# Moving one group of transposed scores ahead of the weighted sums in every second slot of a decoder-layer kernel

## What is computed

```
q = _qdq(x) @ _qdq(wq).T + bq
kv = cond @ wkv.T + bkv                      # cond: 16 x 1500 x 256
attn = softmax(einsum('bnhd,bmhd->bhnm', q, k) * scale, axis=-1)
o = einsum('bhnm,bmhd->bnhd', attn, v).reshape(B, N, C)
```

## Time and profile before

| what | value |
|---|---|
| time, three runs | 882.23, 886.67 and 886.75 us; median 886.67 |
| profiled execution | 884.88 us, span of its instructions 883.1 us |
| mean granted TensorE clock | 0.982 of full |
| PE busy | 800.3 us, 91% |
| DVE busy | 632.6 us, 72% |
| ACT busy | 511.2 us, 58% |
| first and last shift_row (the batches) | 52.4 and 714.3 us from the start |

### The profile page before, as it was taken

One profiled execution on the slowest core, in us unless ns is written; L12 is line 12 of the kernel. 1 busy time (PEld: TensorE's weight loads), 2 busy tenths in 40 slices (PEclk: granted clock), 3 DMA queues, 4 the chain that ended last, 5 costly groups with the idle time before them and its releaser, 6 DMA issues.

```text
span 883.1 us, 30182 instructions
## 1 busy us (share of the span) xinstructions
PE 800.3 (91%) x12379; PEld 608.1 (69%) x12379; DVE 632.6 (72%) x1234; ACT 511.2 (58%) x1084; POOL 260.6 (30%) x334
## 2 busy tenths in 40 slices
PE   5689998999999989999899999999997789999996
PEld 3356766666666666666676666767665569999995
DVE  5866776768777767776777778776864736588887
ACT  2336655666566546655665665656664443687782
POOL 4233223222612251225123421522240103133332
PEclk9999999999999999999999999999999789999999
DMA  7355544554555554554555555545466855766653
GB/s 220 108 149 160 159 137 133 152 164 131 160 148 147 160 149 128 163 152 143 148 151 156 153 158 158 172 136 160 138 190 177 294 195 182 215 202 184 205 155 95
DMA packets 91377, 143.25 MB, mean 162 GB/s; under 512 B 11423, under 2 KB 79583, under 8 KB 87918
## 3 DMA queue, kind: packets, MB, share of 16 engines
q1 hardware_dynamic: 87742, 136.74, 51.8%
q0 software_dynamic: 3504, 4.62, 2.7%
HBM read 101.60 MB, written 39.68 MB: 160 GB/s over the span
## 4 chain that ended last, share of the span: by engine, by line
PE 40%; DMA 29%; DVE 10%; SPq 7%; ACT 7%; issue 5%; DVEq 0%; POOLq 0%; POOL 0%; ACTq 0%
DMA k_dram<-k_two 15%; DMA sums<-y_sb,g_token 9%; PE ps L1613 8%; PE ps L1606 7%; PE ps L1687 5%; SPq L1079 5%; PE ps L1665 4%; DMA k_st<-k_dram 4%; ACT k_two L1368 3%; DVE k_two L507 3%; PE ps L1629 3%; PE ps L1923 3%; DVE negmax L513 2%; PE ps L1944 2%; PE ps L1697 2%
## 5 line engine op out<-in xcount | busy, mean ns | idle before, releaser
L513 DVE TENSOR_REDUCE negmax<-ps 112x1 f32<-112x1500 f32 x121 | 207.3, 1713 | 44.4 <-PE ps L1629 44.1
L1395 ACT ACTIVATE pT<-ps 125x448 f32<-125x448 f32 x384 | 195.8, 546 | 18.6 <-PE ps L1665 14.7
L1230 POOL TENSOR_TENSOR ctx_lo<-ctx_raw,ctx_hi 128x250 f16<-128x250 f32 x188 | 119.3, 666 | 229.7 <-DVE ctx_hi L498 212.8
L1665 PE MATMUL ps<-qbd,k_st 97*128 97x112 f16 x1536 | 129.4, 216 | 20.2 <-ACT qbd L1351 10.8
L1665 PEld LDWEIGHTS ps<-qbd,k_st 97*128 97x128 f16 x1536 | 92.9, 99 | 78.0 <-ACT qbd L1351 27.1
L507 DVE SCALAR_TENSOR_TENSOR k_two<-ps,bk_sb,k_two 128x500 f16<-128x500 f32 x96 | 70.7, 736 | 96.7 <-ACT k_two L1368 96.7
L1368 ACT ACTIVATE k_two<-ps,bk_sb 128x500 f16<-128x500 f32 x96 | 65.1, 678 | 91.6 <-PE ps L1606 68.6
L1351 ACT COPY v_sb<-ps 125x512 f32<-125x512 f32 x96 | 56.3, 587 | 89.5 <-PE ps L1613 89.4
L1687 PE MATMUL ps<-pT,v_sb 125*17 125x56 f32 x6144 | 93.4, 217 | 10.1 <-issue 10.1
L1687 PEld LDWEIGHTS ps<-pT,v_sb 125*17 125x17 f32 x6144 | 81.5, 100 | 29.5 <-issue 19.2
L1629 PE MATMUL ps<-k_st,qbd 96*112 96x500 f16 x363 | 97.4, 375 | 3.7 <-DMA k_st<-k_dram 2.9
(11 more groups left out here) (258 smaller groups left out, 1396.0 us busy)
## 6 DMA issues: line engine op xcount, KB each, us to landing
k_st<-k_dram SPq DMA_DIRECT2D x288, 125.0 KB, 2.6
w_sb<-w SPq DMA_DIRECT2D x25, 1024.0 KB, 5.1
ctx_raw<-ctx_T SPq DMA_DIRECT2D x48, 500.0 KB, 4.5
k_dram<-k_two SPq DMA_DIRECT2D x96, 250.0 KB, 3.6
xs<-zeros SPq DMA_DIRECT2D x28, 260.0 KB, 3.1
w_sb<-w SPq DMA_DIRECT2D x8, 512.0 KB, 4.9
xg<-xs SPq DMA_DIRECT2D x21, 130.0 KB, 4.1
a_x<-x_tok SPq DMA_DIRECT2D x8, 128.0 KB, 2.8
```

What stands on the lines that cost most here:

```text
L513: V.tensor_reduce(negmax[0:QW], ps[0:QW, BANK_S:BANK_S + CHUNKS, 0:MC], AX.XY, ALU.max, negate=True).then_inc(max_done, 1)
L1230: last = nc.gpsimd.tensor_tensor(ctx_lo[:, k, c2, a], ctx_raw[:, k, c2, a], ctx_hi[:, k, c2, a], ALU.subtract)
L1395: nc.scalar.activation(pT[0:MT, (PAIRS * b + p) % 3, TPC * g:TPC * g + TPC], ps[0:MT, BANK_T + n % 2, 0:TPC * QW].rearrange("p (t n) -> p ...
L1665: last = mm(ps[:, BANK_T + n % 2, QW * i:QW * i + QW], k_st[:, j, p, a:a + P], qbd[:, j, p].rearrange("p h s -> p (h s)"), start=True, sto ...
```

## The change

In the fifteen batches with units, group 2 of an odd slot goes to a place behind the unit and in front of the two `pv` on PE. On ACT its exponential goes from behind the next slot's row copy to the end of the same odd slot, behind the unit's copy, `oT_step` and `b_step`. Even slots keep both. No instruction is added or dropped and no DMA is touched.

```
# ACT
-                    if p > 0:
+                    if p > 0 and not (even and units_on):
                         exp_step(b, p - 1, 2)
-                    elif b > 0:
+                    elif p == 0 and b > 0:
                         exp_step(b - 1, PAIRS - 1, 2)
...
                     if even:
                         units(b + 1, 1 - j, us[1:])
+                    elif units_on:
+                        exp_step(b, p, 2)
# PE
                         for u in us:
                             unit(b + 1, 1 - j, u)
+                        if units_on:
+                            scores_T(b, j, p, 2)
                         for q in (p - 2, p - 1):
...
-                    scores_T(b, j, p, 2)
+                    if even or not units_on:
+                        scores_T(b, j, p, 2)
```

## The result

The change makes the kernel slower: 894.03 us in the median of 18 runs (885.73 to 902.82), against 884.18 us for the kernel before in 18 runs beside them. The ratio is 1.0096, with a 95% interval of 1.0069 to 1.0123, about 8.5 us. The forecast was 885.2 us with a range up to 890.6.

The account below looks back on a forecast made before the run. It took PE, busy 91% of the span, as the bound. Terms of -0.6 + 0 + 0 + 0 us gave 884.3 from the profiled run or 886.1 from the median; halfway, 885.2 us, range 880.0 to 890.6.

Parts of the forecast that it names:

- bookkeeping of PE's order: PE in 60 slots: group 2's own time, entering `pv` and leaving `pv`, priced at -0.6, 0 and 0 us.
- Group 2 behind a unit: PE, odd slots: group 2 takes 0.20 us there against 0.21 behind `pv`; at most 0.6 us gained in 60.
- Entering `pv`: PE, start of `pv`: 0.09 us more, paid once before and after the change, so 0.
- Leaving it into shift_row: PE, `pv` directly followed by shift_row: taken as 0, with up to 5.4 us kept for the range; rival's chance 0.06.
- Group 2 never waited at its new place: PE, odd slots: group 2 needs group 0's exponential, ready with 0.8 us to spare; cost 0.
- the moved exponential fitted: ACT: the 0.54 us exponential fits before the next row copy, with 0.35 us left in the tight case; cost 0.
- the rival on issue stalls: PE in `pv`: half of 10.1 us of stalls vanishes (880.1 us, chance 0.07) or is added (890.3 us, chance 0.05).

Follow-up runs that it names:

- act_only: Kernel before with only ScalarE's part of the change: group 2's exponential taken before the next row copy, TensorE's order unchanged; 0.9979 of the kernel before.
- before_again: The kernel before, unchanged, timed against itself as a control; ratio 0.9991.
- thin_before: Kernel before with the weighted sums of only the first head of each pair, so output incomplete; 0.9741 of the kernel before.
- mid_pv: Kernel before with group 2 placed between the two `pv` of an odd slot, ScalarE as before; 1.0141 of the kernel before.
- before_pad8: Kernel before with 4 tiny matmuls (8 TensorE instructions) added in front of everything, while TensorE waits anyway; 1.0083 of the kernel before.
- pe_only: Kernel before with only TensorE's part of the change: group 2 before the weighted sums, ScalarE's order unchanged; 1.0079 of the kernel before.
- thinned kernels: Old and changed order, each with weighted sums of only the first head of each pair; 0.9741 and 0.9702 of the kernel before.

## Why the prediction was wrong

**What held.** Its bookkeeping of PE's order did. Group 2 behind a unit takes 0.01 us less at most, 0.6 us in 60 as summed. Entering `pv` stayed at 0.09 us. Leaving it into shift_row, which no row of before showed, costs 0.035 us in the 46 slots where shift_row comes straight behind `pv`: 1.6 us in all, inside the bounds of 0 and 5.4 that it kept but above the 0 that it took. It took 0 because shift_row was "a full-height transposition as the b_step's are", but the rows have it as 112x97 and those as 128x128. By the Trainium skill's rule on changing the tiling mode (TensorEngine Tiling (Array Packing), Key Properties) the sum was to stay; the trace shows a small price on leaving that depends on what follows (0.035 us in front of shift_row, none in front of the b_step's transposes). Group 2 never waited at its new place. On ACT the moved exponential fitted as worked out: 0.47 us were left in the sixth slot where 0.35 were expected, and act_only costs nothing. Measured in one piece, from the unit's last matmul to the first matmul behind shift_row, the new order is 0.02 to 0.03 us longer in most odd slots without idle time: 1.3 us in 60, 0.14%.

**The step that failed** is the rival on issue stalls: "Nothing ties them to group 2". It gave them 0.05 on the slower side and bounded them by half of the stalls' own length. Two things were wrong.

- *Their number and length are tied to TensorE's stream.* Most stalls sit at fixed instruction numbers (12 of the 14 of the kernel before come back at the same matmul in before_again), and whatever moves code against them draws them anew. The earlier trace rows gave their sum alone.
- *Their price is more than their length.* The bound of half the stalls' length counted idle time alone. In the slots of batch 3 above, 2.1 us of listed idle time cost 5.3 us, since the clock fell behind it.

What the stalls wait for, the traces show too. DMA queue q8 carries packets of 16 KB that the page calls "instruction". Its line in the kernel before and in thin_before:

```profile
q8 instruction: 99, 1.62, 0.8%
```

```profile
q8 instruction: 75, 1.23, 0.6%
```

99 packets for 12379 matmuls and 75 for 9307 are one packet per 125 matmuls and their weight loads in both, and the stalls of the kernel before lie whole multiples of about 124.6 matmuls apart. I set the packets beside the stalls. In the seventeen profiles with the full `pv`, without mid_pv, 217 of the 247 issue stalls over 0.3 us end 1.1 to 1.7 us behind the end of such a packet; 8% of all moments lie so. Of those in `pv` it is 133 of 134. So these stalls are waits for TensorE's code. In batch 3 the kernel before got its packet at 192.82 us, 2.9 us before `pv` began. The changed kernel got it at 197.80, 1.1 us after `pv` had begun, and before_pad8 at 195.90, 1.6 us after.

I then counted over all profiles with the full `pv`: nine of the order before, at its offsets and with act_only, and eight of the changed one, with pe_only (mid_pv left out).

| per profile, over the 120 slots | order before | changed order |
|---|---|---|
| length | 635.0 us | 638.7 us |
| idle, issue | 14.6 us | 15.5 us |
| stalls of 1.4 us or more in odd slots | 18 in 9 | 25 in 8 |
| of these with a lower clock in this slot or the next | 5 | 12 |
| lost to the clock, sum of (1 - PEclk) x slot length | 4.0 us | 6.2 us |
| of this, where PE's longest idle time just before was an issue stall | 2.1 us | 4.3 us |
| of this, where it was a wait for another engine | 1.9 us | 1.9 us |
| waits of PE for other engines | 32.9 us | 33.1 us |

Waits for other engines do not differ. The difference of 3.7 us in length has beside it 0.9 of stalls, 2.2 of clock and 1.3 of direct cost, 4.4 in all. By these means the largest part of what the order costs is the clock behind issue stalls, about two thirds of it behind stalls in `pv` or at the matmul right behind it. But the profiles scatter by some 5 us each. The standard errors are 2.4 us for the 3.7, 1.0 for the 2.2 and 0.9 for the 0.9, so that this split is likely and not shown. It is also smaller than the 0.6% (5.3 us) of the timed runs; the rest is open.

**What stays open.** Why a code packet starts before `pv` in one kernel and only within it in another was not shown, nor why a stall is more often followed by the low clock when group 2 stands in front of `pv`. The thinned kernels, which were to test this, have more slack and don't settle it. 30 of the 247 stalls lie behind no packet as the others do; what they wait for is open.

The range was too narrow for the same two reasons: it took the price of moved code from the stalls' length alone, and the kernel before for a typical draw.

## What to carry to other kernels

When PE is the bound and its stream is long and unrolled, a reordering worth less than 1% can't be judged by one build: time the old and the new order at several offsets (a few idle matmuls in front), and keep the best offset as a gain of its own. Look at the queue of instruction packets beside the issue stalls: whether they are waits for code can be read from the first trace. Price such a stall above its length, since the clock can fall behind it: that was so for 17 of the 43 stalls of 1.4 us or more, and cost 1.7 us more in 15 of them and 3.4 in two. And where a dense run of short matmuls is cut in two, price the second entry: here 0.22 us a time cost 13 us.

## What the hardware showed unexpectedly

- Adding 8 instructions that run while PE is idle made the kernel 0.7 to 0.8% slower in two measurements, 128 of them 1.0%, and 192 nothing (0.9998).
- Stalls put down to issue mostly stay at one instruction number: 3 rows before the end of a `pv` in the kernel before, 7 rows once 8 instructions more stand in front of it, whether these are group 2 or idle matmuls.
- 217 of 247 such stalls end 1.1 to 1.7 us behind the end of a 16 KB instruction packet on q8; by chance 8% would.
- A stall of 2.1 us in `pv` was followed by 5.5 us at a granted clock of 0.51; pairs of unit matmuls started 0.43 us apart there and 0.22 elsewhere. Behind 26 of 43 stalls of 1.4 us or more the clock did not fall.
- The distance from shift_row to the next matmul is 0.05 us behind group 2 and 0.09 us directly behind `pv`.
